# The front of a hybrid attention and feed-forward kernel: maxima and exponentials in a row, another place for the out product, and the last sequence's turn inside the heads

## The reference, cut to what matters

```python
x = x + attn_a(norm(x))   # one head: q, k, v of 1024; scores / sqrt(1024), causal, softmax, out
x = x + ffn(norm(x))      # s = x @ Win + bin; h = relu(s[..., None] * W1 + b1)  (64 x 16)
                          # g = sum(h * W2) + b2;  out = g @ Wout + bout
x = x + attn_b(norm(x))   # 16 heads of 64, causal; inside it a residual and a layer norm
x = x + ffn(norm(x))      # the same weights
```

## Time and profile before

| | us |
|---|---|
| median of 3 runs (lowest, highest) | 846.56 (846.43, 847.8) |
| profiled execution, its own time | 846.91 |
| its span, first to last instruction | 845.0 |
| front, to the first scores of the heads | 203.0 |
| heads, to the end | 642.0 |

### The profile page before, as it was taken

The page is one execution under the profiler, slowest core; times in us unless marked ns, Lnnn a source line. Parts: engine busy times, 40 slices in busy tenths (PEclk is TensorE's granted clock), DMA queues, the critical chain, the costliest instruction groups (busy, mean ns, idle before and its releaser), DMA issues. The chain is left out here.

```text
span 845.0 us, 20974 instructions
## 1 busy us (share of the span) xinstructions
PE 736.2 (87%) x7594; PEld 527.8 (62%) x7594; DVE 629.1 (74%) x1291; ACT 561.1 (66%) x1551; POOL 516.2 (61%) x496
## 2 busy tenths in 40 slices
PE   4887678636999999999999999999999999999752
PEld 3656566533667766766676667667767667676541
DVE  1577766653766688689879877997898699789963
ACT  1466656633767766777777777777777777776633
POOL 3566653531655677666857775785667568666821
PEclk9998888778999999999999999999999999999965
DMA  7500000000798887877778878977787877788720
GB/s 189 127 1 1 0 2 0 1 0 18 146 152 142 146 146 140 145 143 137 144 139 149 148 143 138 153 139 147 141 142 141 145 146 143 151 139 157 136 50 23
DMA packets 360614, 94.00 MB, mean 111 GB/s; under 512 B 347584, under 2 KB 360384, under 8 KB 360512
## 3 DMA queue, kind: packets, MB, share of 16 engines
q1 hardware_dynamic: 357248, 90.57, 59.3%
q10 hardware_dynamic: 3264, 2.10, 0.8%
HBM read 6.63 MB, written 2.10 MB: 10 GB/s over the span
## 5 line engine op out<-in xcount | busy, mean ns | idle before, releaser
L1022 POOL TENSOR_TENSOR prob_hl<-prob,prob_hl 128x768 f16<-128x768 f32 (+1 forms) x192 | 347.4, 1809 | 203.3 <-DVE prob_hl L962 203.1
L933 ACT ACTIVATE prob<-wide,neg_max 128x128 f32<-128x128 f32 (+3 forms) x512 | 264.1, 524 | 157.7 <-DVE neg_max L974 157.6
L974 DVE TENSOR_REDUCE neg_max<-wide 128x2 f32<-128x256 f32 (+3 forms) x256 | 204.6, 820 | 111.7 <-PE wide L851 110.8
L846 PE MATMUL wide<-k_sb,q_sb 64*128 64x128 f32 (+3 forms) x1024 | 190.1, 469 | 0.9 <-ACT k_sb L828 0.8
L962 DVE CAST prob_hl<-prob 128x768 f16<-128x768 f32 (+1 forms) x192 | 155.0, 807 | 0.6 <-ACT prob L933 0.5
L871 PE MATMUL bank<-v_hi,prob_t 128*128 128x64 f16 x1280 | 133.1, 194 | 13.8 <-DMA prob_t<-prob_hl 12.2
L873 PE MATMUL bank<-v_hi,prob_t 128*128 128x64 f16 x1280 | 133.2, 194 | 0.0
L872 PE MATMUL bank<-v_lo,prob_t 128*128 128x64 f16 x1280 | 133.1, 193 | 0.0
L871 PEld LDWEIGHTS bank<-v_hi,prob_t 128*128 128x128 f16 x1280 | 115.8, 98 | 20.6 <-issue 13.7
L873 PEld LDWEIGHTS bank<-v_hi,prob_t 128*128 128x128 f16 x1280 | 114.5, 98 | 0.0
L872 PEld LDWEIGHTS bank<-v_lo,prob_t 128*128 128x128 f16 x1280 | 114.4, 98 | 0.0
(11 more groups left out here) (169 smaller groups left out, 1329.7 us busy)
## 6 DMA issues: line engine op xcount, KB each, us to landing
prob_t<-prob_hl SPq DMA_TRANSPOSE x384, 2.8
x_sb<-in_L_attn_a_in_features SPq DMA_DIRECT2D x8, 256.0 KB, 6.0
out_x<-x_done SPq DMA_DIRECT2D x8, 256.0 KB, 2.5
wq_a<-in_L_attn_a_w_q ACTq DMA_DIRECT2D x1, 512.0 KB, 5.2
wk_a<-in_L_attn_a_w_k ACTq DMA_DIRECT2D x1, 512.0 KB, 6.8
wo_a<-in_L_attn_a_w_o ACTq DMA_DIRECT2D x1, 512.0 KB, 7.5
wv_a<-in_L_attn_a_w_v ACTq DMA_DIRECT2D x1, 512.0 KB, 8.1
wq_b<-in_L_attn_b_Wq SPq DMA_DIRECT2D x1, 512.0 KB, 9.7
```

The lines of the kernel that those rows point to most:

```text
L846: pe.matmul(dst[:, h, c:c + m], q[e, i * P:(i + 1) * P], k[e, 0:m], start=(i == UNIT_ROWS[u][0]), stop=False)
L933: last = act.activation(prob_2[s][:, at:at + m], score_banks(p, s)[:, h, c:c + m], ACT.Exp, bias=neg_max[p % 2][:, h, i:i + 1], accum_out= ...
L974: last = dve.tensor_reduce(neg_max[p % 2][:, :, i:i + 1], score_banks(p, s)[:, :, c:c + m], AX.X, ALU.max, negate=True)
L1022: pool.tensor_tensor(prob_hl[u][:, w:2 * w], prob_2[u][:, 0:w], prob_hl[u][:, 0:w], ALU.subtract)\
```

## The change

- TensorE: the out product goes from the end of step b (sequence b-2, bank TR[1]) to step b+1, behind the scores and the turn of `at_y`; it is now called for b-3 and writes FB, after a wait for the `xt_lo` that reads FB. The turn of unit 2's exponentials comes behind the product for `at_g`. The turn of `y_res` is still last, now behind the first value products, and is left out for the last sequence.
- ScalarE: units 1 and 2 follow with one relu between units 0 and 1 and none between 1 and 2; relu 2 and the following ones come later; the copy of `at_g` comes before the one of unit 2; `xt_hi` is last.
- VectorE: `xt_lo` of b-4 comes first, then the three units' maxima in a row, then `ffn_x_dve` and the statistics, then the adds, the last three together.
- The last sequence's turn, `xt_hi` and `xt_lo` go into the heads: turn and copy in pair (0,1), the subtraction in pair (0,2). TensorE's wait for all `bn_xt_lo` goes from before the heads to the first `output_tensor`.

No operation is added or removed.

```diff
@@ front_tensor, front_turn_* @@
+        def front_turn_tensor(pe, n):
+            wait(pe, "bn_y", n + 1)
+            transposes(pe, FB, y_res[:, seq(n), :].rearrange("p a d -> p (a d)"), QB).then_inc(sem("bn_xt_ps"), 1)
+        def front_turn_scalar(act, n):
+            wait(act, "bn_xt_ps", n + 1)
+            act.copy(xt_hi[:, n * S:(n + 1) * S], FB[:, :]).then_inc(sem("bn_xt_hi"), 1)
+        def front_turn_vector(dve, n):
+            wait(dve, "bn_xt_hi", n + 1)
+            dve.tensor_tensor(xt_lo[:, n * S:(n + 1) * S], FB[:, :], xt_hi[:, n * S:(n + 1) * S].bitcast(F32),
+                              ALU.subtract).then_inc(sem("bn_xt_lo"), 1)
...
                 attn_turn_tensor(pe, b + 1)
+            if turn:
+                wait(pe, "bn_xt_lo", b - 3)
+                ffn_out_pe(pe, FB, b - 3)
             if attn_2:
-                for u in range(NU):
-                    wait(pe, "at_p", NU * b + u + 1)
-                    if u == 1:
-                        wait(pe, "f_x2", b - 2)
...
+                turn_probabilities(0)
+                turn_probabilities(1)
             if attn_1:
                 attn_g_tensor(pe, b + 1)
+            if attn_2:
+                turn_probabilities(2)
...
-            if ffn_2:
-                wait(pe, "at_pt1", min(b + 1, B))
-                wait(pe, "f_x2", b - 2)
-                ffn_out_pe(pe, TR[1], b - 2)
+            if b in FIRST_VALUES:
+                pe.wait_ge(sem("wv_b_lo"), 1)
+                pe.wait_ge(sem("at_x2"), B)
+                for k in FIRST_VALUES[b]:
+                    first_values_tensor(pe, k)
+            if turn and b - 3 < B - 1:
+                front_turn_tensor(pe, b - 3)
@@ front_scalar @@
             for u in range(NU):
-                relus(u)
+                if u < 2:
+                    relus(u)
...
                 turned(act, act.copy, b, 0)
-            relus(3)
+            relus(2)
+            if attn_1:
+                attn_g_scalar(act, b + 1)
             if attn_2:
                 turned(act, act.copy, b, 2)
-            relus(4)
-            if attn_1:
-                attn_g_scalar(act, b + 1)
-            relus(5)
+            relus(3, 4)
             if ffn_1:
                 ffn_x_act(act, SC[2], b - 1)
-            relus(6, 7)
+            relus(5, 6, 7)
@@ front_vector @@
-            if turn:
-                ffn_x_dve(dve, TR[1], b - 3)
-            for u in range(NU):
-                if attn_2:
+            if holds(b, 4, B + 2):
+                front_turn_vector(dve, b - 4)
+            if attn_2:
+                for u in range(NU):
                     wait(dve, "at_s", NU * b + u + 1)
                     row_maxima(dve, SC[u], u, at_neg_max).then_inc(sem("at_m"), 1)
-                if u == 0 and turn:
...
+            if turn:
+                ffn_x_dve(dve, FB, b - 3)
+                wait(dve, "f_x2", b - 2)
+                norm_statistics(dve, b_norm, lambda i: x_sb[:, (b - 3) * QB + i, :], b - 3)
+            adds(0)
             if b == 0:
                 attn_v_vector(dve, 0)
             if attn_2:
                 turned(dve, dve.tensor_copy, b, 1)
-            adds(3)
+            adds(1)
             if norm:
                 front_norm_vector(dve, b + 2)
-            adds(4)
+            adds(2)
             if attn_1:
                 attn_v_vector(dve, b + 1)
-            adds(5, 6, 7)
+            adds(3, 4, 5)
@@ heads_tensor; heads_scalar and heads_vector alike, the latter at s == 1 of (0, 2) @@
             wait(pe, "ctx_t", n + 1)
+            if n == 0:
+                wait(pe, "bn_xt_lo", B)
...
+                if s == 2 and (b, p) == (0, 1):
+                    front_turn_tensor(pe, B - 1)
@@ the blocks @@
             pe.wait_ge(sem("wo_up"), 1)
-            pe.wait_ge(sem("bn_xt_lo"), B)
...
-            front_vector(dve, B + 3)
             over_pairs(dve, heads_vector)
```

More of the change, by code:

```diff
@@ L520, in front_parts, with turn_probabilities @@
                     holds(b, 2, B + 1), holds(b, 3, B + 2))
+        def front_turn_tensor(pe, n):
[8 more added lines that the diff above has]
+                              ALU.subtract).then_inc(sem("bn_xt_lo"), 1)
         def front_tensor(pe, b):
             norm, attn_1, attn_2, ffn_1, ffn_2, turn = front_parts(b)
+            def turn_probabilities(u):
+                wait(pe, "at_p", NU * b + u + 1)
+                if u == 2:
+                    wait(pe, "at_pt0", b + 1)
+                transposes(pe, TR[u % 2], prob[u], len(unit_blocks(u))).then_inc(sem("at_pt_ps"), 1)
             if attn_2 and b > 0:
@@ L579, in front_scalar @@
                 turned(act, act.copy, b, 0)
-            relus(3)
+            relus(2)
+            if attn_1:
+                attn_g_scalar(act, b + 1)
             if attn_2:
                 turned(act, act.copy, b, 2)
-            relus(4)
-            if attn_1:
-                attn_g_scalar(act, b + 1)
-            relus(5)
+            relus(3, 4)
             if ffn_1:
                 ffn_x_act(act, SC[2], b - 1)
-            relus(6, 7)
+            relus(5, 6, 7)
             if ffn_1:
                 ffn_s_act(act, SC[2], b - 1)
-            if turn:
-                wait(act, "bn_xt_ps", b - 2)
-                act.copy(xt_hi[:, (b - 3) * S:(b - 2) * S], FB[:, :]).then_inc(sem("bn_xt_hi"), 1)
+            if b in FIRST_VALUES:
+                for k in FIRST_VALUES[b]:
+                    values_scalar(act, 0, k, VB[k % len(VB)])
+            if turn and b - 3 < B - 1:
+                front_turn_scalar(act, b - 3)
         def front_vector(dve, b):
@@ L623, in front_vector @@
                 turned(dve, dve.tensor_copy, b, 1)
-            adds(3)
+            adds(1)
             if norm:
                 front_norm_vector(dve, b + 2)
-            adds(4)
+            adds(2)
             if attn_1:
                 attn_v_vector(dve, b + 1)
-            adds(5, 6, 7)
+            adds(3, 4, 5)
+            if b in FIRST_VALUES:
+                for k in FIRST_VALUES[b]:
+                    values_vector(dve, 0, k, VB[k % len(VB)])
             if attn_2:
@@ L947, in heads_scalar @@
                     values_scalar(act, b + 1, p, MB)
+                if s == 2 and (b, p) == (0, 1):
+                    front_turn_scalar(act, B - 1)
                 if s == 2 and p == 7 and 0 <= b - 1 < B:
@@ L996, in heads_vector @@
                                       .broadcast_to([P, QB, 2, E]), ALU.mult).then_inc(sem("ctx"), 1)
+                if s == 1 and (b, p) == (0, 2):
+                    front_turn_vector(dve, B - 1)
                 if s == 0:
@@ L1223, in _ @@
                     scale_tensor(pe)
-                if b in FIRST_VALUES:
-                    pe.wait_ge(sem("wv_b_lo"), 1)
-                    pe.wait_ge(sem("bn_xt_lo"), 1)
-                    pe.wait_ge(sem("at_x2"), B)
-                    for k in FIRST_VALUES[b]:
-                        first_values_tensor(pe, k)
             pe.wait_ge(sem("wqk_lo"), 2)
             pe.wait_ge(sem("wo_up"), 1)
-            pe.wait_ge(sem("bn_xt_lo"), B)
             project_tensor(pe, 0, 0, wq_parts, "q_ps")
@@ L1246, in _ @@
                     split_weights_scalar(act)
-                if b in FIRST_VALUES:
-                    for k in FIRST_VALUES[b]:
-                        values_scalar(act, 0, k, VB[k % len(VB)])
             queries_scalar(act, 0, 0)
@@ L1268, in _ @@
                     split_weights_vector(dve)
-                if b in FIRST_VALUES:
-                    for k in FIRST_VALUES[b]:
-                        values_vector(dve, 0, k, VB[k % len(VB)])
-            front_vector(dve, B + 3)
             over_pairs(dve, heads_vector)
```

7 lines of the change are left out of this document (removed).

## The result

The changed kernel takes 822.51 us (median of 4 runs, 822.15 to 822.82), the kernel before beside it 846.88; the ratio is 0.971, with a 95% interval of 0.969 to 0.973. That is 24.4 us less, where 22.1 were forecast. The profiled execution has a span of 820.3 against 845.0.

What follows compares the result with a forecast made beforehand. Front bounded by waits in a ring through three engines, none full; TensorE full in the heads. 20.1 + 0.3 + 2.1 - 0.5 = 22.0 less than 846.91 gives 824.9, as median 824.5 us; range 814 to 836.

Steps and rivals of the forecast that it cites:

- The full step: Front, steps 4 and 5: 15.2 us each after the change, bounded by VectorE and one out product.
- Step 3: Front: 14.6 us, a full step of 15.2 without its `xt_lo`.
- Add 0: VectorE in each front step: taken as 0.5 us, between 0.51 alone and 1.16 beside GpSimd's `ffn_xb`.
- Step 2: Front: 0.3 us less, relieved of the out product's place but with three adds in a row.
- The end of the front: Step 7 to the heads' first scores: a chain of 49.0 us against 51.13, 2.1 less; bounds 43.3 and 52.
- The heads: Three added instructions (turn, `xt_hi`, `xt_lo`) cost 0.5 us, bounds 0 and 1.8.
- rival 5: Heads: last sequence's turn shifts the rhythm, kernel slower, 855 at 0.5 us per pair; sign: outside 642 to 643; chance 0.04.
- Rival 2: TensorE at low clock in each front step: out product 4.8, step 17.1, 9.5 us more, 834; chance 0.12.
- Rival 3: End of the front better or worse than the chain, by its bounds: 819 (chance 0.10) or 827.5 (0.07).
- Rival 4: Front steps: late exponentials hold up VectorE's copy of unit 1; a step of 17 gives 833; chance 0.03.
- Rival 1: Front steps: GpSimd becomes the bound, up to 16.8 per step, five steps 8 us more, 832.5; chance 0.13.
- `at_y` done before the scores' turn: Profile sign in the front: GpSimd finishes `at_y` in time; wrong if TensorE waits for `at_y`.

Runs made afterwards that it cites:

- the fillers: Changed kernel plus 136 identity turns into an unused bank, in TensorE's idle time at the end of the front: 817.84 us, ratio 0.965.
- the doubling: Changed kernel with GpSimd's `ffn_xb` operation done twice in each of steps 1 to 8, once into a spare tile: 831.17 us, ratio 0.981.

## Why the prediction was right

The time was 2.0 below the forecast. In the spans 24.7 went, where the sum had 22.0: 1.2 of the difference is in the five steps, 0.1 at the end of the front and 1.9 in the heads, less 0.5 ahead of step 3. The part in the heads is luck as far as the runs show. By the prediction's own steps:

- **The full step, 15.2.** Steps 4, 5, 6 and 7 took 14.89, 15.25, 13.78 and 14.51, against 15.2, 15.2, 13.9 and 14.5. The wait for the out product was 1.45 for a predicted 1.35, and the adds in a row 0.83 each. The reciprocal's wait, 0.4 of the predicted 1.34 from add 5 to `x_ffn`, is gone (0.94), and step 5 has the 0.37 of waiting for its own statistics. Mechanism and size both hold. The table adds what the prediction didn't say: the 21.3 come with the maxima's part of the change and without the two others. The prediction's "bounded by VectorE and one out product" took the early out product as part of what shortens the step; with the out product at the end the steps take 72.24 as well.
- **Step 3, 14.6.** It took 13.81. Without an `xt_lo` the out product isn't held by it either, and the wait is 0.84, not 1.45: the row of `xt_lo` was subtracted, its effect on TensorE not.
- **Add 0.** 0.5 was right (0.51). That is a gain of its own, since the five adds 0 took 6.47 before (1.10 to 1.64 each) and 2.81 after: 3.7 less of VectorE's busy time, as it no longer works beside `ffn_xb`. The prediction had this inside its 0.5, between bounds of 0.51 and 1.16.
- **Step 2, 0.3 less.** It took 13.14 for 13.04, so the 0.3 wasn't there, and it ended 0.24 later: step 0 ended 1.12 earlier, and step 1 took 12.64 in place of 11.38. That came from TensorE's clock, 0.86 in step 1 and 1.00 before: the row below is the product for `at_g` there, 1.62 where it is 1.13 in a step at full clock. Of the eleven kernels with the maxima in a row, step 1 takes 10.98 in six and 12.64 in five, with the same instructions in it or nearly so.

```profile
36.03 1.62 PE L489 MATMUL bank<-at_x,qk_a 128*128 128x512 f32 x2 [0.60 <-ACT at_x L495]
```

- **The end of the front, 49.0.** It took 48.89, by errors that cancel, and that is luck. From the start of `xt_lo` to VectorE's read of the out product it was 6.27, 6.27 and 5.71, where the sum had 0.6 + 4.8 three times: 2.0 more. The 4.8 was too small by its own rows: the last four products of that one took 0.61, the length that they have at full clock, where the four before took 1.06:

```profile
167.27 1.06 PE L401 MATMUL bank<-w_out,ffn_relu 128*128 128x128 f32 x4
```

  Against it, from the third x_sb to the first scores it was 5.89 (173.84 to 179.73) and not 7.4, as the value products had begun at 173.56, at full clock, where the first of the earlier trace rows took 0.78. The scaling of weights took 0.2 less, and the two stretches from the statistics to the next `xt_lo` 11.72 and 7.37 for 12.0 and 7.6. "The removed turn of the last sequence is largely paid back by out products that now stand inside the chain, three times 4.8" is borne out: with the maxima in a row the turn gives 6.0 to 6.7, the out products take 10.3 to 11.0.
- **The heads, 0.5 more.** They took 1.43 less, outside the 642 to 643 that the prediction named as its sign of being wrong, on the side away from rival 5. The turn itself costs what was said. TensorE's rows around it:

```profile
195.12 0.40 PE L153 MATMUL bank<-wv_b_hi,xt_lo 128*128 128x512 f32 x1
195.36 0.60 PE L185 MATMUL bank<-ident,y_res 128*128 128x128 f32 x4
195.89 0.93 PE L866 MATMUL wide<-k_sb,q_sb 64*128 64x128 f32 x8
```

  It puts the scores back by 0.53. But the heads vary by more, 639.3 to 645.1 over one execution of each of the fourteen kernels, which have the same work in them, with and without the turn; 1.4 of the gain is of that kind, and no experiment here settles where it comes from, nor whether it goes with the kernel or with the execution.

The rivals. Rival 2 (low clock in each step) fell: the clock was 1.00 and out products took 2.99. Rival 3 lay within 0.1 of nothing, though the fillers show that its lower bound was real: with the clock up the end was 42.61, where the prediction's bound for full clock was 43.3. Rival 5 fell: TensorE is busy for all of a 50 us stretch of the heads, as before. Rival 4 fell: VectorE has no second wait of over 0.5 in the five steps.

Rival 1 (GpSimd the bound) fell too, but one of its signs appeared: TensorE did wait for `at_y`, 0.50 once and 0.98 twice, against "`at_y` done before the scores' turn". It cost nothing, since TensorE waited 0.47 and more for `xt_lo` behind it. As a rival the prediction priced only GpSimd slowed by VectorE's adds; the other direction stood in its sum alone, in the choice of 0.5 for add 0. The doubling showed what that one can cost: VectorE slowed by GpSimd, an add of 0.51 at 1.53, and VectorE is the engine in the ring. The Trainium skill, GPSIMD Engine Reference, section "8. Key points", has GpSimd share its SBUF interfaces with VectorE and contend with instructions there that have two SBUF inputs or are in a 2-port mode. The runs agree for the adds, which read two tensors: GpSimd's y operations took 1.73 alone, 2.26 beside one add and the start of another, and 3.28 beside more of them. Add 0 reads one tensor, and no row shows its mode. From the changed kernel, steps 5 and 7:

```profile
95.00 2.26 POOL L364 TENSOR_SCALAR y_res<-x_sb,bn_neg_mean,bn_rstd 128x128 f32<-128x128 f32 x4
...
99.83 1.73 POOL L364 TENSOR_SCALAR at_y<-x_sb,at_neg_mean,at_rstd 128x128 f32<-128x128 f32 x4
...
125.63 3.28 POOL L364 TENSOR_SCALAR y_res<-x_sb,bn_neg_mean,bn_rstd 128x128 f32<-128x128 f32 x4
```

The 16.8 of that rival needed 3.28 for both norms of a step. In steps 3 to 5 the b norm had 2.25 or 2.26 and the first norm 1.73; in steps 6 and 7, where it had 3.26 and 3.28, there is no first norm.

What stays open: the spread of the heads, the chance of the low clock in step 1, the share of the clock in the steps' gain, and which of the rearrangements that come with the maxima are needed.

## What to carry to other kernels

When a change has several parts, price each in every stretch that it runs through: here a part worth nothing in the steady steps cost 11 us where the pipeline drains, because the bank it used tied it to another chain (`xt_lo`). Before an instruction is moved into a wait, ask which buffer it needs and who empties it; an early place with the other bank was worth 17 us, and the end of the front, where the place was the same, gave 13. And where an engine in the ring works beside another on SBUF, look at the length of its rows as well as at its waits: a step can grow by 1.0 with no wait longer than before.

## What the runs showed of the hardware

- VectorE's tensor_scalar of 128x512 (add 0) took 0.51 alone. Where it ran beside a tensor_tensor of GpSimd and 0.3 or more of that was still to come, it ended 0.28 to 0.33 after the end of that one: in the rows of the doubling above GpSimd's second operation ends at 96.47 and add 0 at 96.76, 0.29 later; in the earlier trace rows add 0 ends at 101.12, and GpSimd's `ffn_xb` beside it (99.51, 1.28 long) at 100.79. It holds in the five steps of the kernel before (1.10 to 1.64) and in step 3 of the changed one (0.74). So the add did some 0.2 of its 0.51 beside GpSimd's operation, and no more however long the two stood side by side. It didn't get between two of them either: in step 3 of the doubling it began at 62.94 beside the first (62.15 to 63.43), the second ran from 63.38 to 64.66, and the add ended at 64.97. In step 3 of the kernel before it began first, at 61.80 against 61.89, and still ended 0.28 after GpSimd. POOL's times are rough.
- Three VectorE adds of which each reads the one before took 2.48, 0.83 each, where one with another instruction between takes 0.66 of distance.
- 136 identity turns on an otherwise idle TensorE raised the mean granted clock of 50 us from 0.69 to 0.97 and shortened a waiting chain by 6.3.
- The same instructions in step 1 took 10.98 in some kernels and 12.64 in others, with TensorE at the low clock in part of it in the latter (0.86 or 0.87 over the step, 1.00 in the former). The five of 12.64 had ended step 0 at 32.6 to 32.8, the six of 10.98 at 33.2 to 35.1, and step 1 ended at 45.3 to 45.5 and at 44.2 to 46.0. A step read by itself can differ by 1.7 us for that alone; in the time it may not show.
